# Counting sort of a graph kernel: stores over 128 partitions, taken from the tables, in a written-out loop

## What is computed

```python
def reference(x, src, dst, edge_attr_64, edge_weight, ...):
    edge_index = jnp.stack([src, dst])
    h = jnp.maximum(_layernorm(x, axis=-1), 0.0)
    x = x + _L0_gnn_ref(h, edge_index, edge_weight, ...)   # 2 rounds: sum over edges of weight * h[src] into dst
    h = jnp.maximum(_layernorm(x, axis=-1), 0.0)
    x = x + _L1_gnn_ref(h, edge_index, edge_attr_64, ...)  # attention, 4 heads, scores also from the edge features
    h = jnp.maximum(_layernorm(x, axis=-1), 0.0)
    x = x + _L2_gnn_ref(h, ..., src, dst)                  # attention, 8 heads
    h = jnp.maximum(_layernorm(x, axis=-1), 0.0)
    x = x + _L3_gnn_ref(h, edge_index, ...)                # 2 rounds: sum over edges with a tanh gate
    return x
```

## Time and profile before

| | us |
|---|---|
| median of 3 runs | 5874.53 |
| lowest, highest | 5868.89, 5880.49 |
| profiled execution, its own time | 5883.4 |
| its span in the trace | 5881.6 |
| POOL busy | 3279.7 (56% of the span) |
| VectorE (DVE) busy | 2412.2 (41%) |
| TensorE (PE) busy | 2235.2 (38%) |
| ScalarE (ACT) busy | 686.5 (12%) |
| the 400 stores, L447, busy on POOL | 518.7 |

### The profile page before, as it was taken

The page is one execution under the profiler, slowest core; times in us unless marked ns, Lnnn a source line. Parts: engine busy times, 40 slices in busy tenths (PEclk is TensorE's granted clock), DMA queues, the critical chain, the costliest instruction groups (busy, mean ns, idle before and its releaser), DMA issues. The chain is left out here.

```text
span 5881.6 us, 56887 instructions
## 1 busy us (share of the span) xinstructions
PE 2235.2 (38%) x14712; PEld 1848.8 (31%) x14713; DVE 2412.2 (41%) x5041; ACT 686.5 (12%) x1814; POOL 3279.7 (56%) x3006
## 2 busy tenths in 40 slices
PE   7220036665323334444404445545405223342332
PEld 7110025554222223443401244444303222232322
DVE  7650046555334433333475333333584322322323
ACT  2010012222000022222201111111201000000000
POOL 2887767774767625555441444444251667636775
PEclk9995556666555565555555555555555555655556
DMA  4001121112111212222341222222340111121112
GB/s 119 8 6 6 6 59 45 43 44 34 47 45 46 42 36 69 73 73 73 86 129 48 82 89 88 88 88 88 90 144 31 51 46 46 46 32 46 46 46 45
DMA packets 173165, 342.94 MB, mean 58 GB/s; under 512 B 69874, under 2 KB 95719, under 8 KB 172828
## 3 DMA queue, kind: packets, MB, share of 16 engines
q0 software_dynamic: 99328, 193.92, 14.8%
q1 hardware_dynamic: 67586, 135.53, 6.8%
q10 hardware_dynamic: 6170, 12.57, 0.6%
HBM read 266.34 MB, written 73.24 MB: 58 GB/s over the span
## 5 line engine op out<-in xcount | busy, mean ns | idle before, releaser
L466 POOL DMA_INDIRECT rows<-tab_dram,tblk x1248 | 1247.9, 1000 | 811.1 <-issue 365.8
L466 POOL DMA_INDIRECT big<-tab_dram,tblk x832 | 831.8, 1000 | 1070.1 <-DVE rows L1356 601.5
L845 PE MATMUL bank<-rows,OH 128*128 128x128 f32 x3328 | 749.9, 412 | 1748.6 <-issue 414.9
L845 PEld LDWEIGHTS bank<-rows,OH 128*128 128x128 f32 x3328 | 690.4, 314 | 1797.0 <-issue 1596.8
L1252 DVE TENSOR_TENSOR ACC<-ACC,bank 128x128 f32 x1664 | 477.2, 287 | 1253.1 <-remote 861.6
L447 POOL DMA_INDIRECT rec_dram<-stg_rec,stg x400 | 518.7, 1297 | 224.9 <-issue 223.4
L466 POOL DMA_INDIRECT rows<-tab_dram,big x416 | 470.6, 1131 | 165.5 <-issue 120.7
L925 PE MATMUL bank<-rows,OH 128*128 128x132 f32 (+1 forms) x1664 | 373.5, 407 | 387.8 <-ACT S L631 291.5
L925 PEld LDWEIGHTS bank<-rows,OH 128*128 128x128 f32 x1664 | 341.9, 304 | 414.1 <-ACT S L631 288.3
L1176 DVE TENSOR_TENSOR OH<-iota,recS 128x1024 f32<-128x1024 f32 (+1 forms) x260 | 318.3, 1225 | 180.6 <-issue 170.8
L476 POOL TENSOR_TENSOR big<-big,MT 128x1056 f32<-128x1056 f32 (+1 forms) x104 | 209.8, 2019 | 288.6 <-DMA big<-part_dram 190.0
(11 more groups left out here) (246 smaller groups left out, 3880.2 us busy)
## 6 DMA issues: line engine op xcount, KB each, us to landing
part_dram<-S SPq DMA_DIRECT2D x52, 544.0 KB
big<-part_dram SPq DMA_DIRECT2D x52, 544.0 KB, 3.6
part_dram<-S SPq DMA_DIRECT2D x52, 528.0 KB
big<-part_dram SPq DMA_DIRECT2D x52, 528.0 KB, 3.5
rows<-tab_dram,tblk POOLq DMA_INDIRECT x1248
big<-tab_dram,tblk POOLq DMA_INDIRECT x832
HN<-in_edge_attr_dram ACTq DMA_DIRECT2D x23, 500.0 KB
rows<-tab_dram,big POOLq DMA_INDIRECT x416
```

The lines of the kernel that those rows point to most:

```text
L466: nc.gpsimd.indirect_dma_start(to[:, q, j, :], None, tab_dram[k], bass.IndirectOffsetOnAxis(ap=idx[:, G * g + j:G * g + j + 1], axis=0)).t ...
L845: last = nc.tensor.matmul(bank[4 + 2 * (q % 2) + j // 4][:, (j % 4) * P:(j % 4 + 1) * P], OH[:, q, j, :], rows[:, q, j, :], start=True, st ...
```

## The change

Each store names all 128 partitions. The record table is cleared over 128 partitions (`rec_all`), and the row table too has 128 (`row_all`): two new VectorE instructions give the three lanes without edges row numbers behind the sorted part, and `rec_dram` gets 3 x 400 rows more to hold their records. The stores take records and row numbers straight from these tables; the staging buffers, SP's copies into them and the semaphores `s_sstage` are gone. POOL's loop is written out, 400 stores in 50 groups of eight. POOL now waits itself for `s_placed`, for the edge scores of its group (`s_esc`), and, from the third group on, for the stores of the group two before, so that at most 16 are under way; three semaphores `s_scat` take turns for that.

```diff
@@ -105,7 +105,8 @@
             return ctx.enter_context(nc.semaphore(name))
 
 
-        rec_dram = nc.dram_tensor("rec_dram", (P * TILES, REC), F32).ap()
+        rec_dram = nc.dram_tensor("rec_dram", (P * TILES + (P - LANES) * COLS, REC), F32).ap()
+        rec_rows = rec_dram[0:P * TILES, :].rearrange("(p t) r -> p (t r)", p=P)
         tab_dram = [nc.dram_tensor(f"tab{k}_dram", (N, WIDTH[k]), F32).ap() if k in WIDTH else None for k in range(len(PASSES))]
         part_dram = [nc.dram_tensor(f"part{k}_dram", (GROUPS, P, G * (D + HEADS[k])), F32).ap() for k in sorted(LOADED)]
 
@@ -157,7 +158,8 @@
         blk_i = sb("blk_i", [P, TILES], I32)
 
         MT = sb("MT", [P, TILES * H])
-        rec = MT[0:LANES, 0:COLS * REC].rearrange("p (c r) -> p c r", r=REC)
+        rec_all = MT[:, 0:COLS * REC].rearrange("p (c r) -> p c r", r=REC)
+        rec = rec_all[0:LANES, :, :]
         e_dst = FT[0:LANES, 0:COLS].bitcast(I32)
         e_src = FT[0:LANES, COLS:2 * COLS].bitcast(I32)
         e_w = FT[0:LANES, 2 * COLS:3 * COLS]
@@ -167,7 +169,9 @@
         e_sloc = ACC[0:LANES, 2 * COLS:3 * COLS]
         e_pos = ACC[0:LANES, 3 * COLS:4 * COLS]
         e_rank = ACC[0:LANES, 4 * COLS:5 * COLS]
-        e_row = ACC[0:LANES, 5 * COLS:6 * COLS].bitcast(U32)
+        row_all = ACC[:, 5 * COLS:6 * COLS].bitcast(U32)
+        e_row = row_all[0:LANES, :]
+        spare = sb("spare", [P, 1])
         tot = sb("tot", [LANES, NB])
         base_pos = sb("base_pos", [LANES, NB])
         tcount = sb("tcount", [P, 4, NB])
@@ -179,8 +183,6 @@
         ea = hn1[0:LANES, 0:2048].rearrange("p (a f) -> p a f", a=2)
         eaT = hn1[:, 2048:2048 + 8 * LANES].rearrange("p (a f) -> p a f", a=2)
 
-        stg = sb("stg", [P, 2, G], U32)
-        stg_rec = sb("stg_rec", [LANES, 2, G, REC])
         rows = sb("rows", [P, RING, G, D])
         wide = {k: big[:, 0:RING * G * WIDTH[k]].rearrange("p (a t f) -> p a t f", a=RING, t=G) for k in KEPT}
         iota_i = rows[:, 0, 0:4, :].rearrange("p a f -> p (a f)").bitcast(I32)
@@ -257,8 +259,7 @@
         s_eaTc = sem("s_eaTc")
         s_es = sem("s_es")
         s_esc = sem("s_esc")
-        s_sstage = [sem(f"s_sstage{i}") for i in range(2)]
-        s_scat = [sem(f"s_scat{i}") for i in range(2)]
+        s_scat = [sem(f"s_scat{i}") for i in range(3)]
         s_hoh = sem("s_hoh")
         s_hmm = sem("s_hmm")
         s_hacc = sem("s_hacc")
@@ -372,21 +373,11 @@
             sp.dma_start(X[:, 0:NB - 1, :], x[0:(NB - 1) * P, :].rearrange("(b p) f -> p b f", p=P)).then_inc(s_load_x, 16)
             sp.dma_start(X[0:TAIL, NB - 1, :], x[(NB - 1) * P:N, :]).then_inc(s_load_x, 16)
             sp.wait_ge(s_recdef, 1)
-            sp.dma_start(rec_dram.rearrange("(p t) r -> p (t r)", p=P), recS[:, :, :].rearrange("p t r -> p (t r)")).then_inc(s_recinit, 16)
-
-            sp.wait_ge(s_placed, 1)
-            for i in steps(sp, COLS // 16):
-                for half in range(2):
-                    sp.wait_ge(s_esc, 2 * i + half + 1)
-                    sp.sem_inc(s_gate, 1)
-                    if not isinstance(i, int):
-                        sp.wait_ge(s_scat[half], 16 * G * i)
-                    sp.dma_start(stg_rec[:, half, :, :], rec[:, bass.ds(G * (2 * i + half), G), :]).then_inc(s_sstage[half], 16)
-                    sp.dma_start(stg[0:LANES, half, :], e_row[:, bass.ds(G * (2 * i + half), G)]).then_inc(s_sstage[half], 16)
-
-            for half in range(2):
-                sp.wait_ge(s_scat[half], 16 * G * (COLS // 16))
-            sp.dma_start(recU.rearrange("p t r -> p (t r)"), rec_dram.rearrange("(p t) r -> p (t r)", p=P)).then_inc(s_recl, 16)
+            sp.dma_start(rec_rows, recS[:, :, :].rearrange("p t r -> p (t r)")).then_inc(s_recinit, 16)
+
+            for r in range(3):
+                sp.wait_ge(s_scat[r], 16 * G * ((COLS // G - 1 - r) // 3 + 1))
+            sp.dma_start(recU.rearrange("p t r -> p (t r)"), rec_rows).then_inc(s_recl, 16)
 
             TABS = {0: TAB[:, :, 0:D], 1: TAB[:, :, 0:D], 2: TAB[:, :, 0:D + 4],
                     4: QKV[:, :, D:3 * D], 6: TAB[:, :, 0:D], 7: TAB[:, :, 0:D]}
@@ -439,14 +430,15 @@
             nc.gpsimd.iota(lane_i[:, :], pattern=[[0, 1]], base=0, channel_multiplier=1).then_inc(s_iota, 1)
 
             pool.wait_ge(s_recinit, 16)
-            for i in steps(pool, COLS // 16):
-                for half in range(2):
-                    pool.wait_ge(s_sstage[half], 32 * (i + 1))
-                    pool.sem_inc(s_gate, 1)
-                    for j in range(G):
-                        nc.gpsimd.indirect_dma_start(
-                            rec_dram, bass.IndirectOffsetOnAxis(ap=stg[0:LANES, half, j:j + 1], axis=0),
-                            stg_rec[:, half, j, :], None).then_inc(s_scat[half], 16)
+            pool.wait_ge(s_placed, 1)
+            for g in range(COLS // G):
+                pool.wait_ge(s_esc, g + 1)
+                if g >= 2:
+                    pool.wait_ge(s_scat[(g - 2) % 3], 16 * G * ((g - 2) // 3 + 1))
+                for c in range(G * g, G * g + G):
+                    nc.gpsimd.indirect_dma_start(
+                        rec_dram, bass.IndirectOffsetOnAxis(ap=row_all[:, c:c + 1], axis=0),
+                        rec_all[:, c, :], None).then_inc(s_scat[g % 3], 16)
             pool.wait_ge(s_recl, 16)
 
             for k in GATHERED:
@@ -1051,7 +1043,9 @@
 
 
             dve.wait_ge(s_load_e, 48)
-            link(v.memset(rec[:, :, :], 0.0))
+            link(v.memset(rec_all[:, :, :], 0.0))
+            link(v.tensor_scalar(spare[:, :], lane[:, :], float(COLS), float(P * TILES - LANES * COLS), ALU.mult, ALU.add))
+            link(v.tensor_scalar(row_all[:, :], iota[:, 0:COLS], spare[:, 0:1], None, ALU.add))
             dve.sem_inc(s_recbase, 1)
             for ends, blk, loc in ((e_dst, e_blk[:, :], rec[:, :, R_DST]), (e_src, e_sblk[:, :], e_sloc[:, :])):
                 link(v.tensor_single_scalar(e_int[:, :], ends[:, :], 7, ALU.arith_shift_right))
```

## The result

| | before | after |
|---|---|---|
| median of 4 runs, us | 5874.59 (5868.89 to 5880.49) | 6044.98 (6034.10 to 6051.97) |
| span of the profiled execution, us | 5881.6 | 6043.2 |
| last store, us | 743.94 | 657.47 |
| first gather, us | 760.00 | 924.63 |

The changed kernel is slower: ratio 1.0288, 95% interval 1.0270 to 1.0307. The forecast was 5774 us. The stores did what was forecast, and yet the first gather starts 164.6 us later.

A forecast was written before the change was run, and what follows sets the result against it. POOL's stores were taken to bound the path, up to 315 us of them standing alone. Shorter stores and an earlier start end them 101 us sooner: 5883.4 to 5782, less 8.9 for the median run, 5774 us; range 5740 to 5820.

The forecast's parts named there:

- One store: POOL's sort stores: 128 partitions spread like a gather, 0.944 us instead of 1187 ns, so 1.25 us from one to the next.
- The start: Start of the sort: no staging copy before POOL's first store, which comes at 100.2 instead of 104.9, 4.7 us gained.
- Beside VectorE: Stores beside VectorE's histogram loop: its compares hold some, six fit an 8.87 us iteration, 147 from 160 to 378 us.
- The last store: End of POOL's sort stores: the last ends at 644 instead of 745.1 us, 101 us less.
- The wait for landing: POOL's wait in each store group for the group two before: lag at most 4.90 us against 10 us, costs nothing.
- The sum's last step: From last store to first gather and behind: nothing changes, the same 14.87 us, first gather near 659.
- The rivals: Store cases: length goes with direction (12%), five per iteration (10%), seven (5%), half the saving (7%), landing becomes the bound (4%).
- the slower one (landing): POOL's wait at each group's head: landing becomes the bound; at 20 us lag the kernel takes 5979 us; 4%.

The follow-up runs named there:

- e5: The changed kernel with stores over 126 partitions instead of 128; 6057.07 us against 5877.58 for the kernel before.
- e1: The changed kernel with its stores over the 125 partitions that hold records; 5881.75 us against 5882.96 for the kernel before.
- e9: The changed kernel with at most two stores under way instead of 16; 5789.47 us against 5842.60 for the kernel before.
- e10: The changed kernel with a small POOL memset and a wait for it after each store; 5790.98 us against 5842.60 for the kernel before.
- e14: The changed kernel with a small POOL memset and wait after each of the first 192 stores; 5755.85 us against 5841.91 for the kernel before.
- e3: The kernel before with POOL's store loop alone written out, 125 partitions and staging copies kept; 5894.01 us against 5882.96 for the kernel before.
- e18: The changed kernel with memset filler after the first 192 stores and, in the two keeping passes, seven of eight gathers; 5618.55 us, ratio 0.9557 to the kernel before.
- e7: The changed kernel with two instead of four products per group of edge scores, half the scores left out; 6042.49 us against 5877.58 for the kernel before.
- e13: The changed kernel with a small POOL memset and wait after each of the first 48 stores only; 5972.57 us against 5841.91 for the kernel before.
- e16: The changed kernel with stores over the first 64 partitions only, the other records left out; 6171.22 us against 5841.91 for the kernel before.
- e6: The changed kernel with 125 partitions in the first 21 store groups and 128 after; 5830.06 us against 5877.58 for the kernel before.

## Why the prediction was wrong

- **One store**: right, and so is the reason given for it, the division of the rows. 0.944 us was forecast, 958 ns came, in sixteen equal pieces of 256 bytes; 126 partitions, which go into 14 pieces, took 984 ns (e5). The Trainium skill's page (DMA: Bandwidth & Descriptors, section Anatomy of one DMA — SWDGE (gpsimd) path) would have left the 1187 ns as they were; the runs disagree with it: 1187 to 1190 ns for 125 partitions, 958 for 128, 895 for 64.
- **The start**: right. 100.2 us was forecast, 99.3 came, and 99.4 in e1.
- **Beside VectorE**: void here. In the changed kernel no histogram ran, and 173 stores passed between 160 and 378 us for 147 forecast. Six stores to an iteration were seen where the histogram did run: in e9 (147), and with filler in e10 and e14 (146 to 147).
- **The last store**: 657.5 + 0.95 = 658.4 for 644, 14 us off, by two errors that partly cancel: POOL twice waited for edge scores, 28.7 us together, of which the forecast had nothing, and no compare held the stores.
- **The wait for landing**: costs nothing, as forecast, and so, as far as can be told, does the written-out loop (e3: 5894 against 5883, 0.2% apart, one run each, with the histogram beginning at 158.4).
- **The sum's last step failed**: "After it nothing changes: the same 14.87 us lead to the first gather", and with it "ScalarE's edge scores … stay ahead of the stores". Both took VectorE's 429.4 us as fixed. It became 915.6 us, because TensorE and VectorE crawl beside stores that follow at 1.26 us. The error, 5774 against 6045, is nearly all in that step: the first gather came at 924.6 instead of 659, 266 us late. POOL's wait behind the last store was 266.2 us instead of 14.87, which makes 251 us of it; the other 14 us are the later last store. With filler behind the stores until the histogram was done (e14) the same path gave 672.8 against the forecast 659, and 86 us gained (one run) against 101.
- **The rivals**: the slower one (landing) did not happen; none had other engines slowed by the stores. The trace of before had a warning, which the prediction did not use. In the fourth pass its gathers follow each other at 1.25 us, and beside them ScalarE's copy of a transpose waits without a named releaser, 23 times and 286.4 us together, like this:

```profile
3819.46 0.28 ACT L606 ACTIVATE dlT<-bank 128x128 f32<-128x128 f32 x1 [11.83 <-remote]
```

What stays open is which shared part the stores fill up. It is shown to set in with the number of indirect DMAs per us (a mean step of 1.29 us brings it, one of 1.48 us does not), and not to go with their rows, addresses, direction, the number under way, the waits on them or the loop that issues them. DMA engines 5% busy and landings that never held POOL up speak against the DMA engines themselves. Loads of instructions do not show as the cause either: between 160 and 378 us the instruction queue moved one packet in the changed kernel. The Trainium skill (NOTIFIC — the notification-queue block, section Overflow: three behaviours, one of which stalls the engine) states that the block which writes the trace's records holds an engine back rather than lose a record inside itself. By that rule the crawl could be a cost of recording. No run here shows it either way: every time of this study comes with a recorded span, so it is not known whether the crawl, and the gain from pacing, are there without one. A plain limit on the DMA packets recorded does not fit. Between 160 and 378 us the DMA views have, in the kernel before at full speed and in the changed one in the crawl:

```profile
DMA packets 7836, 1.18 MB, mean 5 GB/s; under 512 B 7221, under 2 KB 7836, under 8 KB 7836
```

```profile
DMA packets 5895, 2.26 MB, mean 10 GB/s; under 512 B 5519, under 2 KB 5519, under 8 KB 5894
```

A limit on the packets of POOL's own queue would fit (3936 before, 4672 in e10, 5504 in the crawl), and no run parts it from a limit on the stores themselves.

## What to carry to other kernels

When a change makes one engine issue faster, ask what that rate does to the engines beside it, and look for a row in which the new rate has already been held beside the same work; a count that fits in the sum is not such a row. If the work beside it stalls without a releaser ("remote", "issue") and short register instructions grow to 0.70 us, try pacing the issuer: here 0.15 us of filler between indirect DMAs turned 170 us of loss into 86 us of gain (e14, one run), and with the gathers of two passes paced too the gain was 4.4% (e18).

## What the runs showed of the hardware

- Beside indirect DMAs of POOL at a mean step of 1.25 to 1.29 us (64, 126 or 128 partitions, either direction) TensorE's results came at one matmul with its weight load per 2.80 us, for matmuls of different shapes (e7, e13, e16), and VectorE's register instructions lasted up to 0.70 us; at a mean step of 1.48 us (e9, e10) the same loops ran at or near full speed.
- In the crawl the trace books matmuls long before their results are there: a burst over at 273.4 us was waited for until 292.02 and 303.12.
- The crawl begins some 15 us after the first store on VectorE, not at once, and in stretches where other engines have little to do it costs nothing (e6, the end of e14).
- POOL's time for an indirect store went with how the partitions divide, hardly with their number: 125 in 1187 to 1190 ns, 126 in 984, 128 in 958, 64 in 895.
